# First attention: the scores of a query's two key tiles joined into one square of 128 columns

## The reference, cut to what matters

```python
q, k, v = heads of x @ wq, x @ wk, x @ wv
q, k = _rope(q, pos), _rope(k, pos)
scores = jnp.einsum('bqhgd,bshd->bhgqs', qg, k) * sm_scale
allowed = (j <= i) & (j > i - SLIDING_WINDOW)          # i query, j key, window 128
attn = jax.nn.softmax(jnp.where(allowed, scores, neg), axis=-1)
out = jnp.einsum('bhgqs,bshd->bqhgd', attn, v).reshape(...) @ wo
```

## Time and profile before

| what | us |
|---|---|
| median of 3 runs (lowest, highest) | 1131.33 (1128.28, 1136.68) |
| the profiled execution | 1129.72 |
| its span in the trace | 1128.0 |
| PE busy in the span | 1095.9 (97%) |
| DVE, ACT, POOL busy | 731.3, 636.4, 458.0 |

### The profile page before, as it was taken

How to read it: one execution, slowest core, us unless ns; L and a number is a source line. 1 busy time by engine, 2 the same in 40 slices (tenths; PEclk the granted TensorE clock), 3 DMA queues, 4 the chain that set the end, 5 groups by cost and what they waited for, 6 DMA issues and landing times. The chain is left out here.

```text
span 1128.0 us, 19366 instructions
## 1 busy us (share of the span) xinstructions
PE 1095.9 (97%) x6266; PEld 899.1 (80%) x6266; DVE 731.3 (65%) x2384; ACT 636.4 (56%) x1487; POOL 458.0 (41%) x471
## 2 busy tenths in 40 slices
PE   7899999999999999999999999999999999999997
PEld 5788888888888888888888877888888865555786
DVE  6767776667776657776667776222233588997675
ACT  6656665556665556666566564454410237778424
POOL 4654554354544344553445251333310326445300
PEclk9999999999999999999999999999999988999999
DMA  6011110011110011110100001222200246661002
GB/s 240 20 38 38 38 39 29 13 38 39 38 38 28 13 47 39 38 29 29 29 28 20 29 1 38 68 81 74 86 1 4 37 51 84 91 111 19 1 1 75
DMA packets 28566, 49.72 MB, mean 44 GB/s; under 512 B 4400, under 2 KB 5552, under 8 KB 28464
## 3 DMA queue, kind: packets, MB, share of 16 engines
q1 hardware_dynamic: 27888, 47.41, 17.3%
q10 hardware_dynamic: 576, 1.05, 0.3%
HBM read 38.35 MB, written 2.10 MB: 36 GB/s over the span
## 5 line engine op out<-in xcount | busy, mean ns | idle before, releaser
L497 POOL TENSOR_TENSOR turned<-turned,sin 128x512 f32<-128x512 f32 x73 | 94.6, 1296 | 309.8 <-ACT turned L357 309.8
L373 ACT ACTIVATE probs<-probs,neg_max 128x256 f32<-128x256 f32 (+1 forms) x256 | 119.9, 474 | 11.4 <-DVE neg_max L590 11.4
L1748 DVE CUSTOM_DVE_ANT_0 a_unused<-bank,a_mask 128x512 bf16<-128x512 f32 (+3 forms) x256 | 108.9, 487 | 6.6 <-PE bank L1964 6.0
L500 POOL TENSOR_TENSOR turned<-turned,by_cos 128x512 f32<-128x512 f32 x73 | 101.1, 1385 | 5.7
L96 PE MATMUL bank<-wo_hi,oT_hi 128*128 128x512 f32 x256 | 100.3, 392 | 1.6 <-DVE oT_lo L653 1.6
L744 PE MATMUL bank<-xT_hi,wq_hi 128*128 128x512 f32 x256 | 101.6, 397 | 0.0
L744 PE MATMUL bank<-xT_lo,wq_hi 128*128 128x512 f32 x256 | 100.2, 391 | 0.0
L744 PE MATMUL bank<-xT_hi,wq_lo 128*128 128x512 f32 x256 | 100.1, 391 | 0.0
L96 PE MATMUL bank<-wo_hi,oT_lo 128*128 128x512 f32 x256 | 99.9, 390 | 0.0
L96 PE MATMUL bank<-wo_lo,oT_hi 128*128 128x512 f32 x256 | 99.7, 390 | 0.0
L432 ACT ACTIVATE pT_hi<-bank 128x512 fp32r<-128x512 f32 x112 | 61.7, 596 | 51.7 <-PE bank L783 51.7
(11 more groups left out here) (246 smaller groups left out, 3173.7 us busy)
## 6 DMA issues: line engine op xcount, KB each, us to landing
staged<-weights SPq DMA_DIRECT2D x70, 256.0 KB, 2.7
f_staged<-weights_f SPq DMA_DIRECT2D x33, 256.0 KB, 2.7
a_q_stack<-a_qT_hi SPq DMA_DIRECT2D x32, 128.0 KB, 3.4
rows<-x_rows SPq DMA_DIRECT2D x2, 1024.0 KB, 7.3
a_q_stack<-a_qT_lo SPq DMA_DIRECT2D x16, 128.0 KB, 3.9
out<-rows SPq DMA_DIRECT2D x8, 256.0 KB, 2.0
a_raw<-weights_qkv SPq DMA_DIRECT2D x4, 384.0 KB, 4.8
probs<-weights SPq DMA_DIRECT2D x4, 256.0 KB, 5.1
```

The lines of the kernel that those rows point to most:

```text
L373: act.activation(probs[:, s % 2, h, 0:width], probs[:, s % 2, h, 0:width], ACT.Exp, bias=neg_max[:, s % 2, h:h + 1], scale=SCALE0, accum_o ...
L497: pool.tensor_tensor(at, at, sin[:, :], ALU.mult).then_inc(sin_done, 1)
L500: pool.tensor_tensor(at, at, by_cos_at(a, first), ALU.add).then_inc(roped, 1)
L1748: dve.tensor_tensor_reduce(unused[:, UNUSED_AT[qt]:UNUSED_AT[qt] + seen], ps_s[bank][:, at:at + seen], mask[:, SEQ - seen:SEQ], 1.0, LOWES ...
```

## The change

A slot with two key tiles is now a joined slot: there are 12 in a pair and 48 in all. Its scores are still made for 256 columns. ACT copies the 128 columns of the query's own tile out of PSUM (`copy_scores`, two instructions), DVE writes the other tile's scores over them where the mask says so (`copy_predicated`, two instructions), and one reduction finds the four maxima. Exponentials, `normalise` (one instruction now, by a multiplication of two tensors, for all heads) and transposes (four) work on 128 columns. The turned square is then parted by 0/1 masks: high half times the earlier tile's mask, high half times the own tile's mask, and the same two for the low half (`whole_lo`). Three of these four multiplications are DVE's and the fourth (`own_low`) POOL's; in the closing slots 9 to 15 POOL also has the own high half (`own_high`) and `normalise` of slots 12 to 15. `apply_probs` takes the earlier tile's high half first and waits for the four parts one after another.

The order changes too: a single piece is projected whole ahead of `apply_probs`, `project_out` of a slot moves behind the work of the next slot (slot 15 has that of 14 and its own), ACT turns the piece ahead of the output's copy and copies values ahead of the exponentials. Two weights of the start are staged in another place.

```diff
+def joined_before(s):
+    return (s // 4) * 3 + max(0, s % 4 - 1)
+JOINED = joined_before(SLOTS)
 
...
-        probs = sb("probs", [P, 2, GROUP0, 2 * P])
+        probs = sb("probs", [P, 2, GROUP0, P])
+        whole_lo = sb("whole_lo", [P, GROUP0, P])
...
+            def copy_scores(i, s):
+                if s % 4 == 0:
+                    return
+                for pair in range(2):
+                    act.wait_ge(scored, 2 * (SLOTS * i + s) + pair + 1)
+                    act.activation(probs[:, s % 2, 2 * pair:2 * pair + 2, :], scored_keys(pair, 1), ACT.Copy).then_inc(copied, 1)
...
             def slots(i, last=False):
                 for s in range(CLOSING if last else SLOTS):
                     high_probs(i, s)
+                    for later in scores_ahead(s, last):
+                        copy_scores(i, later)
                     for a in pieces_before(s, last):
                         rope_high(i, a)
                     pieces = pieces_of(s, last)
-                    if len(pieces) == 2:
-                        turn(i, pieces[0])
+                    turn(i, pieces[0])
                     high_output(i, s)
+                    for tile in values_in(s, last):
+                        high_values(i, tile)
                     for later in scores_ahead(s, last):
                         exps(i, later)
-                    for tile in values_in(s, last):
-                        high_values(i, tile)
-                    for a in pieces[-1:]:
+                    for a in pieces[1:]:
                         turn(i, a)
                     for w in weights_of(s, last):
                         split_weight(i, *w)
...
+            def own_low(i, s):
+                pool.wait_ge(pT_lo_done, SLOTS * i + s + 1)
+                pool.tensor_tensor(by_head(pT_lo[:, 1, :]), whole_lo[:, :, :], each_head(own_kept),
+                                   ALU.mult).then_inc(own_lo_done, 1)
+            def own_high(i, s):
+                own = by_head(pT_hi[:, 1, :])
+                pool.wait_ge(parted, 3 * (JOINED * i + joined_before(s)) + 1)
+                pool.tensor_tensor(own, own.bitcast(F32), each_head(own_kept), ALU.mult).then_inc(parted, 1)
             def slots(i, last=False):
-                for s in range(SLOTS):
+                for s in range(CLOSING if last else SLOTS):
+                    if s % 4:
+                        own_low(i, s)
                     for a in pieces_of(s, last):
                         rotate(i, a)
...
-                width = key_tiles(s % 4)[1] * P
                 pool.wait_ge(inv_done, SLOTS * i + s + 1)
-                for h in range(GROUP0):
-                    pool.tensor_scalar(probs[:, s % 2, h, 0:width], probs[:, s % 2, h, 0:width], inv_sum[:, s % 2, h:h + 1],
-                                       None, ALU.mult).then_inc(probs_done, 1)
+                pool.tensor_tensor(probs[:, s % 2, :, :], probs[:, s % 2, :, :], scales(s), ALU.mult).then_inc(probs_done, 1)
 
             with pool.Fori(0, PAIRS - 1) as i:
                 slots(i)
             slots(PAIRS - 1, last=True)
-            for s in range(CLOSING + AHEAD0 + 1, SLOTS):
-                normalise(PAIRS - 1, s)
+            for s in range(CLOSING, SLOTS):
+                if s % 4:
+                    own_high(PAIRS - 1, s)
+                    own_low(PAIRS - 1, s)
+                if s + AHEAD0 + 1 < SLOTS:
+                    normalise(PAIRS - 1, s + AHEAD0 + 1)
...
+                else:
+                    for pair in range(2):
+                        dve.wait_ge(copied, 2 * (JOINED * i + joined_before(s)) + pair + 1)
+                        dve.copy_predicated(probs[:, s % 2, 2 * pair:2 * pair + 2, :],
+                                            each_head(own_added.bitcast(U32), 2),
+                                            scored_keys(pair, 0)).then_inc(masked, 2)
+                    dve.wait_ge(masked, GROUP0 * (SLOTS * i + s + 1))
+                    dve.tensor_reduce(row_max[:, s % 2, :], probs[:, s % 2, :, :], AXIS.X, ALU.max).then_inc(peaked, 1)
+                    dve.wait_ge(peaked, JOINED * i + joined_before(s) + 1)
                 dve.tensor_scalar(neg_max[:, s % 2, :], row_max[:, s % 2, :], -SCALE0, None,
                                   ALU.mult).then_inc(max_done, 1)
...
-                width = key_tiles(s % 4)[1] * P
-                for h in range(GROUP0):
-                    dve.tensor_scalar(probs[:, s % 2, h, 0:width], probs[:, s % 2, h, 0:width], inv_sum[:, s % 2, h:h + 1], None,
-                                      ALU.mult).then_inc(probs_done, 1)
+                dve.tensor_tensor(probs[:, s % 2, :, :], probs[:, s % 2, :, :], scales(s), ALU.mult).then_inc(probs_done, 1)
...
-            def low_probs(i, s):
-                for kb in range(key_tiles(s % 4)[1]):
-                    dve.wait_ge(pT_hi_done, 28 * i + blocks_before(s) + kb + 1)
-                    dve.tensor_tensor(pT_lo[:, kb, :], ps_t[kb][:, :], pT_hi[:, kb, :].bitcast(F32),
-                                      ALU.subtract).then_inc(pT_lo_done, 1)
+            def low_probs(i, s, own=True):
+                high, bank = by_head(pT_hi[:, 1, :]), by_head(ps_t[0][:, :])
+                low = whole_lo[:, :, :] if s % 4 else by_head(pT_lo[:, 1, :])
+                dve.wait_ge(pT_hi_done, SLOTS * i + s + 1)
+                dve.tensor_tensor(low, bank, high.bitcast(F32), ALU.subtract).then_inc(pT_lo_done, 1)
+                if s % 4 == 0:
+                    return
+                done = 3 * (JOINED * i + joined_before(s))
+                dve.tensor_tensor(by_head(pT_hi[:, 0, :]), high.bitcast(F32), each_head(earlier_kept),
+                                  ALU.mult).then_inc(parted, 1)
+                if own:
+                    dve.wait_ge(parted, done + 1)
+                    dve.tensor_tensor(high, high.bitcast(F32), each_head(own_kept), ALU.mult).then_inc(parted, 1)
+                dve.wait_ge(pT_lo_done, SLOTS * i + s + 1)
+                dve.tensor_tensor(by_head(pT_lo[:, 0, :]), whole_lo[:, :, :], each_head(earlier_kept),
+                                  ALU.mult).then_inc(parted, 1)
...
-                    add_output(i, s, last)
+                    if s >= 1:
+                        add_output(i, s - 1, last)
+                    if s == SLOTS - 1:
+                        add_output(i, s, last)
...
-            def turn_probs(i, s, last):
...
-            def apply_probs(i, s):
+            def turn_probs(i, s):
+                pe.wait_ge(probs_done, SLOTS * i + s + 1)
+                for h in range(GROUP0):
+                    mm = pe.transpose(ps_t[0][:, h * P:(h + 1) * P], probs[:, s % 2, h, :], ident[:, :])
+                mm.then_inc(pT_ready, 1)
+            def apply_probs(i, s, closing=False):
 
                 u, qt = divmod(s, 4)
                 g, b = divmod(u, 2)
...
+                at = slice(g * P, (g + 1) * P)
+                earlier, own = b * SEQ_TILES + qt - 1, b * SEQ_TILES + qt
+                steps = [(v_hi[:, own, at], pT_hi[:, 1, :]), (v_lo[:, own, at], pT_hi[:, 1, :])]
+                steps.append((v_hi[:, own, at], pT_lo[:, 1, :]))
+                if qt:
+                    steps.insert(0, (v_hi[:, earlier, at], pT_hi[:, 0, :]))
+                    steps.insert(1, (v_lo[:, earlier, at], pT_hi[:, 0, :]))
+                    steps.insert(4, (v_hi[:, earlier, at], pT_lo[:, 0, :]))
+                if s >= 1:
+                    pe.wait_ge(o_lo_done, SLOTS * i + s)
+                done = 3 * (JOINED * i + joined_before(s))
+                if qt == 0:
+                    pe.wait_ge(pT_lo_done, SLOTS * i + s + 1)
+                else:
+                    pe.wait_ge(parted, done + 1)
+                for n, (v, p) in enumerate(steps):
+                    if qt and n == 2:
+                        pe.wait_ge(parted, done + (3 if closing else 2))
+                    if qt and n == 4:
+                        pe.wait_ge(parted, done + 3)
+                    if qt and n == 5:
+                        pe.wait_ge(own_lo_done, JOINED * i + joined_before(s) + 1)
+                    mm = pe.matmul(ps_o[:, :], v, p, start=(n == 0), stop=(n == len(steps) - 1))
+                mm.then_inc(o_ready, 1)
...
                 pe.wait_ge(o_lo_done, SLOTS * i + s + 1)
+                if s >= 1:
+                    pe.wait_ge(y_added, SLOTS * i + s)
                 three(pe, ps_y[:, :], [(oT_hi[:, s % 2, h * P:(h + 1) * P], oT_lo[:, s % 2, h * P:(h + 1) * P],
...
                 for s in range(CLOSING, SLOTS):
                     if s == CLOSING:
-                        turn_probs(i, s, True)
+                        turn_probs(i, s)
                         scores(i, s + AHEAD0)
-                    apply_probs(i, s)
+                        project_out(i, s - 1)
+                    apply_probs(i, s, True)
                     if s + 1 < SLOTS:
-                        turn_probs(i, s + 1, True)
```

(35 more changed lines are left out.)

76 lines of the change are left out of this document (37 added, 39 removed).

## The result

The changed kernel takes 1166.51 us (median of 4 runs, 1163.61 to 1168.60) against 1132.01 (1128.28 to 1136.68) of the kernel before: ratio 1.031, 95% interval 1.028 to 1.034. It is slower, as forecast, but by 34.5 us where the forecast was 16.4, and 2.5 us above the stated range. The profiled execution has a span of 1166.9 us (before: 1128.0) at a mean granted clock of 0.972 (before: 0.991). It was the slowest of its four, that of before 2.3 us under its median, so the spans differ by 38.9 us where the medians differ by 34.5; what is read from the traces adds up to 38.9.

The account below looks back on a forecast made before the run. The prediction took TensorE's own work to bound the attention loop, busy 586.18 of 592.00 us. Its terms, -16.5 + 17.6 + 2.3 + 13 = +16.4 us on the profiled 1129.72, gave 1146 us, range 1117 to 1164.

Parts of the forecast that it names:

- transposes, 38 slots: Joined slots in the loop: four transposes instead of eight save 0.435 us in each of 38 slots, -16.5 us.
- parts and ports: Joined slots: VectorE and GpSimd exclude each other at shared SBUF ports, delaying the turned square's parts; +17.6 us, bounds 0 to 49.
- slots 0 and 1 with the head: Slot 0 loses 2.73 us, slot 1 waits for `wk_lo`; less transposes and earlier waits, net +2.3 us (-6 to +8).
- closing slots: GpSimd's own parts queue behind a later slot's `normalise`; slots 10, 11 and 13 lose 4.3 us each, +13 us (0 to 30).
- the walk: One joined slot followed engine by engine from its first transpose: losses of 5.2 us per pair, 2.5 of them in slot 10.
- the 18 that the forecast gave as a sign: In the loop, TensorE's waits on VectorE's masks and GpSimd's `own_low` would sum to about 18 us.
- The second rival: Joined slots: the parts fit into gaps and stalls fall to about nothing; -4.5 us, so 1125; chance 0.27.
- `project_out` one slot later: Slot 0 is 2.73 us shorter but its weights no sooner; slot 1 waits 2.3 us, plus 0.8 for late parts, four times.
- The third rival: Closing slots: in addition GpSimd's order does not bind, costing +3 instead of +13 us; 1115 in all; chance 0.13.
- The fourth: Joined slots: VectorE becomes the bound, 10.4 us against 8.7 in some 20 slots; +30 or more, 1174; chance 0.08.

Follow-up runs that it names:

- the two kernels across pairs: Slot 15's `project_out` moved into the next pair's slot 0: on the changed kernel with two GpSimd edits, 1118.64 us; on the kernel before, scores not joined, 1132.70 us.
- joined scores across pairs: Changed kernel with slot 15's `project_out` in the next pair's slot 0, VectorE making own low outside closing slots, GpSimd's own parts ahead of a later normalisation: 1118.64 us.
- The experiment on own low: Changed kernel, with VectorE instead of GpSimd making the own low part outside the closing slots: 1156.08 us, ratio 1.020 to the kernel before.
- the run with own parts first: Changed kernel, with GpSimd making slot s + 1's own parts ahead of normalising slot s + 3 in the closing slots: 1151.22 us, ratio 1.017 to the kernel before.

## Why the prediction was right in direction and wrong in size

Each term as forecast and as the slots' lengths in the trace give it (after less before, with the moved `project_out` of 2.73 put back). In slots 2 to 15 before's joined slots are taken 0.435 shorter, so the first row is set by this and not measured:

| term | forecast | trace |
|---|---|---|
| transposes, 38 slots | -16.5 | -16.5 (set) |
| parts and ports, slots 2 to 14 | +17.6, with slot 15 | +12.5 |
| slots 0 and 1 with the head, net of their transposes | +2.3 | +8.5 |
| slot 15 | in parts and ports, 0.2 to 0.8 a pair | +16.0 |
| closing slots | +13 | +15.7 |
| behind the attention | 0 | +2.8 |
| sum | +16.4 | +39.0 (spans: 38.9) |

*Transposes*: right, at 0.36 from four transposes to the next instruction. In the two kernels across pairs, slots that differ by four transposes and show no wait give 0.11 to 0.12 for one. The figure of the Trainium skill (TensorE: Matmul & The Clock Gate, Back-to-back issue gap), which would have made the term 12.3, was further off.

*Parts and ports*: the mechanism was right and named in its place (own low between own high and the rest, 1.66 for 0.69); the walk was too high by 5 us. Slot 10 lost 1.4, not 2.5. TensorE's waits on the parts in the loop are 4.4 us, not the 18 that the forecast gave as a sign. Another 5.6 us lie in 53 matmuls of `apply_probs` that come about 0.34 us after the one before at full clock, with no wait shown for them; for 41 the weight load waited for one of VectorE's parts. With joined scores across pairs 12 such matmuls are left. The experiment on own low confirms the mechanism for some 8 of the 12.5: the same instruction of VectorE takes 1.66 us beside GpSimd's own low and 0.76 without it. The rule of the Trainium skill (SBUF — State Buffer, Who interferes with whom), a VectorE instruction with two SBUF inputs against a GpSimd one that reads SBUF, agrees with these two numbers. The second rival, no stalls, is refuted for the changed kernel, but is what the version with own low on VectorE nearly does.

*`project_out` one slot later*: this is the step that failed. The wait that it worked out for slot 1, 2.3 us on `wk_lo`, was measured at 2.28, partly by luck: both its ends came 0.5 to 0.6 us later than worked out. But the step counted only the slot from which `project_out` leaves, not the one into which the last is pushed. Slot 15 has two products on one PSUM bank, and the sum that frees it is queued on VectorE behind an instruction that waits for ScalarE. Slot 15 costs 16.0 us in three pairs, most of the 22.6 that the forecast misses by the spans: 10.9 are the wait on `rows`, 3.6 the low clock. Moving the sum gave 9.2 of it back, and letting `project_out` cross to the next pair all of it (slot 15 at 10.15). The prediction names `add_output` as something that delays the parts, not as something that TensorE waits for. The head's pair also waited 4.1 for `wk_lo` rather than 2.3.

*The clock*: the second omission, spread over the terms. In the attention of before the granted clock is 1.00 throughout, of after it is 0.50 for 41 us in all, always at or behind one of the three waits. There 66 matmuls of 512 columns came 0.427 us apart instead of 0.227; with transposes and scores that is 17.5 us of work at half speed: 8.4 in slots 0 and 1, 3.6 in slot 15, 5.4 in the closing slots. The forecast priced each wait at its own length. In slots 0 and 1 the 8.4 are more than the whole miss of 6.2.

*Closing slots*: right in mechanism and nearly in size, 12.4, 12.6 and 11.2 for the three slots instead of 11.1. In slot 10 GpSimd's `normalise` begins 8.2 us after the first transpose instead of 7.1, and the last matmuls of the slot run at the low clock. The third rival, GpSimd's order not binding, is refuted, and by the edit that makes it true: 15.3 us back, 13.1 of the profiled difference in these slots. The fourth, VectorE as the bound, is refuted by own low on VectorE: more work there, 10.4 us less time.

What stays open: *behind the attention* nothing was forecast, and 2.8 us are there, 1.3 of them a longer wait of TensorE for `f_xT_lo` (2.0 instead of 0.7). Slot 10 keeps about 1.1 us above TensorE's work in the best version, behind slot 9 with its two weights; moving a weight was not tried.

## What to carry to other kernels

When work is moved one step later in a loop, price both ends: the step that becomes too short to cover its loads, and the step that gets it twice; the cure here was to let it cross the loop's edge. Take a list's order as a cost of its own: an instruction that two engines wait for does not belong behind one that waits for a third, and moving one line in GpSimd's list was worth 13 us or more. Count a wait of TensorE at more than its length where a stretch at the low clock follows: here 17.5 of 39 us. Where VectorE reads two SBUF tensors, giving GpSimd a share of the same chain may cost more than doing it all on VectorE.

## What the runs showed of the hardware that was not expected

TensorE's clock did not fall at a fixed point of a wait. In slot 15 of the first pair it fell 1.5 us after the end of the 3.64 us of waiting: six matmuls ran at 0.23 us, and only then did they come at 0.43. In the slot 1 that follows it fell 0.3 us before the wait of 2.28 ended, and the matmuls behind it were slow at once:

```profile
216.70:218.18 1.48, 1.48 (x7) 1.24 (x8) 0.00 (x0) 0.00 (x0) 0.00 (x0) 1.00 0.04 11
218.18:220.67 2.49, 2.49 (x8) 1.77 (x6) 0.00 (x0) 0.00 (x0) 0.00 (x0) 0.50 0.00 0
```

The same slot 1 was at 14.1 to 14.3 us in the second to fourth pair of the changed kernel, but at 13.1 in the same pairs of the run with own parts first, where nothing in that slot was edited, the wait is the same and the clock stayed at 1.00:

```profile
230.98 0.49 PE L808 MATMUL bank<-xT_hi,wk_hi 128*128 128x512 f32 x1 [2.28 <-POOL wk_lo L564]
```

Whether a wait of this length is followed by the low clock is not settled by the wait alone. GpSimd's multiplication with the four row scales read over the columns took 1.04 us, that with a 128x128 mask read for each head 1.26, at the same 128x512.
